# Ten and seven edge columns instead of eight and five for a tile of a relational graph layer

## The reference

```python
msgs = x[src]
out = x @ root + bias
for r in range(8):
    mask = (edge_type == r).astype(x.dtype)
    sums = jax.ops.segment_sum(msgs * mask[:, None], dst, num_segments=n)
    cnt = jax.ops.segment_sum(mask, dst, num_segments=n)
    out = out + (sums / jnp.maximum(cnt, 1.0)[:, None]) @ weight[r]
```

## Time and profile before

| | |
|---|---|
| three runs | 1642.74, 1644.76, 1646.51 us |
| profiled execution | 1644.54 us, its span 1642.8 us |
| PE busy | 1554.4 us (95% of the span), 7138 matmuls |
| VectorE busy | 890.7 us (54%) |
| GpSimd busy | 809.8 us (49%) |
| ScalarE busy | 406.0 us (25%) |
| items | 180: 130 planes (1580), 50 left-over columns (1564) |
| granted clock of PE | 0.987 of full speed over the span |

### The profile page before, as it was taken

How to read it: one execution, slowest core, us unless ns; L and a number is a source line. 1 busy time by engine, 2 the same in 40 slices (tenths; PEclk the granted TensorE clock), 3 DMA queues, 4 the chain that set the end, 5 groups by cost and what they waited for, 6 DMA issues and landing times.

```text
span 1642.8 us, 19045 instructions
## 1 busy us (share of the span) xinstructions
PE 1554.4 (95%) x7138; PEld 1259.3 (77%) x7138; DVE 890.7 (54%) x1334; ACT 406.0 (25%) x595; POOL 809.8 (49%) x682
## 2 busy tenths in 40 slices
PE   4999999999999999999999999999999879997988
PEld 4987777777778678888887888888777758876887
DVE  6535222444442320003888888884667656877785
ACT  3321112222222112122222222222211123232320
POOL 4426766667663136545555565654655634232220
PEclk9999999999999999999999999999999989998999
DMA  4422323333333222226777788877889874540001
GB/s 160 144 89 80 92 79 94 108 98 102 95 90 112 71 78 99 84 88 222 263 254 255 245 276 281 278 242 240 301 285 317 287 257 163 186 148 0 39 39 49
DMA packets 120459, 262.48 MB, mean 160 GB/s; under 512 B 23451, under 2 KB 37010, under 8 KB 120360
## 3 DMA queue, kind: packets, MB, share of 16 engines
q1 hardware_dynamic: 48568, 109.34, 19.9%
q0 software_dynamic: 33056, 83.02, 16.6%
q10 hardware_dynamic: 38736, 68.83, 11.3%
HBM read 193.33 MB, written 80.06 MB: 166 GB/s over the span
## 4 chain that ended last, share of the span: by engine, by line
PE 63%; DVE 16%; issue 8%; DMA 6%; POOL 3%; ACT 2%; ACTq 0%; POOLq 0%; SPq 0%; DVEq 0%
PE ps L1831 49%; DMA source_rows<-relation_rows,row_list 6%; PE ps L2074 5%; PE ps L2083 2%; DVE u_sum L1580 2%; PE ps L1958 1%; PE ps L1914 1%; PE ps L1938 1%; PE ps L1950 1%; POOL source_rows L922 1%; POOL xf L1025 1%; DVE u_sum L1590 1%; ACT source_rows_hi L2292 1%; PE ps L2144 1%; DVE xf L1726 1%
## 5 line engine op out<-in xcount | busy, mean ns | idle before, releaser
L1831 PE MATMUL ps<-WH,XTH 128*128 128x512 f32 (+1 forms) x1680 | 666.9, 397 | 0.0
L1831 PE MATMUL ps<-WH,XTL 128*128 128x512 f32 (+1 forms) x1680 | 652.6, 388 | 0.0
L1831 PE MATMUL ps<-WL,XTH 128*128 128x512 f32 (+1 forms) x1680 | 652.5, 388 | 0.0
L864 POOL TENSOR_TENSOR WL<-RAW,WH 128x512 fp32r<-128x512 f32 (+1 forms) x184 | 243.6, 1327 | 289.4 <-ACT WH L2210 286.4
L1831 PEld LDWEIGHTS ps<-WH,XTH 128*128 128x128 f32 x1680 | 318.4, 190 | 65.6 <-issue 7.1
L1831 PEld LDWEIGHTS ps<-WH,XTL 128*128 128x128 f32 x1680 | 316.7, 189 | 64.8
L1831 PEld LDWEIGHTS ps<-WL,XTH 128*128 128x128 f32 x1680 | 317.6, 189 | 60.7 <-issue 2.4
L922 POOL DMA_INDIRECT source_rows<-relation_rows,row_list x180 | 221.6, 1231 | 235.4 <-DVE u_sum L1580 130.7
L2232 ACT ACTIVATE EV<-ps 128x512 f32<-128x512 f32 x180 | 107.6, 598 | 631.6 <-PE ps L1831 543.2
L943 POOL DMA_INDIRECT edge_lists<-edge_words x160 | 196.9, 1231 | 46.4 <-issue 44.2
L1580 DVE SCALAR_TENSOR_TENSOR u_sum<-source_rows,weight_list,u_sum 128x1024 f32<-128x1024 f32 x120 | 165.4, 1378 | 60.8 <-DMA source_rows<-relation_rows,row_list 55.7
(11 more groups left out here) (312 smaller groups left out, 1499.9 us busy)
## 6 DMA issues: line engine op xcount, KB each, us to landing
relation_rows<-EV ACTq DMA_DIRECT2D x160, 256.0 KB
RAW<-in_L_gnn_weight SPq DMA_DIRECT2D x128, 256.0 KB
u_rows<-u_sum SPq DMA_DIRECT2D x20, 512.0 KB
RAW<-in_L_gnn_w_gate SPq DMA_DIRECT2D x32, 256.0 KB
mix_rows<-mix_rows_out ACTq DMA_DIRECT2D x10, 512.0 KB, 2.6
root_rows<-EV ACTq DMA_DIRECT2D x20, 256.0 KB
u_sum<-u_rows SPq DMA_DIRECT2D x10, 512.0 KB
bias_rows<-root_rows SPq DMA_DIRECT2D x10, 512.0 KB, 6.5
```

Of the source, the lines that this page charges most:

```text
L864: g.tensor_tensor(WL[:, h % 2, k, 0:w], RAW[:, q % 4, 0:w], WH[:, h % 2, k, 0:w].bitcast(F32), ALU.subtract).then_inc(w_lo, 1)
L1831: mm = t_.matmul(ps[:, bank, 0:w], a[:, t, k, :], b[:, s, k, 0:w], start=(k == 0 and j == 0), stop=(k == KT - 1 and j == 2))
```

## The change

Two tuples change. Everything that is computed from them moves with them: the number of items (130 + 50 = 180 becomes 170 + 30 = 200), the columns of the lists (180 becomes 200), the places of the left-over columns in a tile (0 and 6 of 12 in the first group, 0 of 8 in the second), the step of every item and of every fetch, and `COUNTED_AT` (88 becomes 85).

```diff
-PLANES = (8, 5)
-OVER = (3, 2)
+PLANES = (10, 7)
+OVER = (2, 1)
```

## The result

The change makes the kernel 0.8% slower: 1658.5 us, median of 7 runs (1653.0 to 1663.1), against 1645.5 for the kernel before in the same session; the ratio is 1.0082, 95% interval 1.0067 to 1.0098, +13 us. The forecast was 1640.2 with a range up to 1655. The profiled execution of the changed kernel took 1661.1 us, its span is 1659.3, 16.5 us longer than that of before.

What follows compares the result with a forecast made beforehand. PE was taken to bound most of the first group, the items the second. -2.9 - 5.9 + 1.5 + 1.0 + 2.0 = -4.3 us on 1644.5 gave 1640.2 us; range 1626 to 1655, the forecast's own 1635 to 1646.

Steps and rivals of the forecast that it cites:

- Counting, -2.9: Counting of left-over edges: 20 of 50 small PE matmuls go, all on the path, -2.9 us.
- PE's part, -5.9: First group, 881 to 1113 us: 6.3 left-over columns go where PE is the bound, -5.9 us.
- VectorE in the first group, +1.5 and +1.0: First group's added VectorE work: +1.5 us of PE waits from 881 to 1113, +1 us from 750 to 881.
- my sign for a wrong reading: First group's end shifting over 3 us against 9 us of PE work saved would prove that stretch misread.
- The fetches and the four slots in the second group, +2: Second group: 20 more fetches for the same rows through four slots, +0.2 us a tile, +2 us; ends -33 and +31.
- the long way round: Second group: a slot's 11.5 us from release after the second plane to use of its rows; as bound, +0.7 us a tile.
- the rest of the tile: Second group: the removed column's 1.9 us of VectorE and its waits go there, counting where another way is the bound.
- the first rival: Second group: slots become the bound twice a tile, group grows by 15 us, 1653 us; smaller form 1646; chance 0.29.
- My upper end of +31: Second group: if each fetch keeps its 3.09 us share, a tile takes 24.7 us, ten tiles +31 us.
- Moves the wait and doesn't add one: Group's end: seven planes, not three, follow the last left-over column; PE waits at the end instead, no added time.
- The rule: Fixed 2.0 us a DMA: 20 more fetches bring 40 us, 10 us with four in flight; sum would be 1643.
- The second (VectorE the bound of the first group, 0.08): First group: VectorE becomes the bound, 5.9 us lost and 3 us added, 1648 us; chance 0.08.

Runs made afterwards that it cites:

- the blocks cut: 24 quantizing blocks on VectorE cut to 16 of 352 columns: 1635.3 us on the changed kernel, 1639.4 us on the kernel before.
- the emptied fetches: Full change, four slots, with fetches of the first group's ninth and tenth and second group's sixth and seventh planes moving almost no rows: 1651.1 us.

## Why the prediction was wrong, step by step

The sum was -4.3 us and the spans differ by +16.5. Of the 20.8 us between them 12.2 lie in the first group, 8.2 in the second and 0.4 in the start.

**Counting, -2.9.** Right: 20 matmuls, 2.9 us.

**PE's part, -5.9, and VectorE in the first group, +1.5 and +1.0.** These three make -3.4; measured +8.8, and my sign for a wrong reading came, the group's end moved by 6.2 us. PE's columns did go (with the blocks cut, the first group fell from 360.0 to 350.6, the 9.3 us of ten columns). The step that failed is "what it needs is about ... 217.5 of 226 us. That holds on the mean". I compared VectorE's total with the stretch, and left out the slots in this group altogether; I had named the blocks that bunch VectorE's work and priced them at 1.5. The runs put in its place: 24 blocks of 4.4 to 7.3 us stop all releases, four slots cover no more than four items, and the loop's 7.3 us from release to landed begin again behind them. With 12 items a tile the group loses 23.5 us against PE's need, where 11 items lost 5.4, and a fifth slot gives 14 of them back. That there is no time between blocks to catch up is how I read this; one place of the trace was followed.

**The fetches and the four slots in the second group, +2.** Measured +8.7 in nine tiles and 1.5 at the end. The step that failed is the last one: I had +0.7 us a tile from the long way round, and let "the rest of the tile" give back nearly all, to +0.2. A tile grew by 0.97 (21.58 to 22.55). The long wait did not settle at the sixth plane: the longest of a tile stands there in four tiles and at the fourth, fifth or seventh plane in the others, and is 5.0 us or more in four of ten; two such waits in a tile, the sign of the first rival, show in none, but there are 21 waits and not 13. I took off 0.5 us for 31 fewer edges. By the emptied fetches this was too much: 1202 rows less gave this group 7 us, 0.006 us a row and not 0.017. What a tile saves elsewhere helps little where slots turn round twice a tile. The mean loop of the earlier trace rows was there to be read: seven items in 21.6 us with four slots is 12.3 us a loop. My upper end of +31 took this loop as fixed; it shortened from 12.45 to 11.53 us, 0.7 since rows wait less for VectorE and 0.6 since they land sooner, against 0.4 lost in the release and the fetch.

**"Moves the wait and doesn't add one"** at the end of the group: 1.5 us, small.

**The rule** of the Trainium skill ("DMA: Bandwidth & Descriptors", "Anatomy of one DMA — SWDGE (gpsimd) path"), about 2.0 us fixed in a DMA: the trace agrees in one place, where an empty tenth plane lands 1.88 us behind its instruction, and shows more in the three others (3.15, 5.57 and 4.50 us). It is a sixth of the loop, and priced alone it gave 1643.

**The rivals.** The first (slots the bound, second group +15, chance 0.29) is what the second group did, at two thirds of its price. The second (VectorE the bound of the first group, 0.08) came at the same time and cost more than its 3 us; its sign as I wrote it, VectorE without idle time, did not show. The range failed because I let only one of them happen at a time, though both feed on the same added items.

## What to carry to other kernels

Before items are added to a ring, read the loop of a slot from the trace (release, issue, landing, turn, use), divide by the slots, multiply by the new number of items, and compare that with the stage, in every stage that uses the ring. A block of other work on the consumer of the ring can count twice, once as work and once as a latency that starts again behind it, when it is longer than the slots can cover: here 24 blocks cost 23.5 us with four slots and 12 items a tile. Trading matrix work for items pays where the number of items stays (9, 5 with 2, 2: -5 us with four slots, and -11 with five, 1631.2 to 1619.8). A slot more (4 KB a partition) gave -14 us before the change and -29 after it, and with it the change neither pays nor costs (1631.2 and 1629.0).

## What the runs showed of the hardware

A gather's time from the end of its instruction to the landing hardly follows its rows. In the first group of the changed kernel the first left-over column of a tile (128 rows) takes 4.3 us, the second (27 on the mean) 4.5, the tenth plane (68) 3.7; emptied, that plane takes 1.9, but the second group's sixth plane still 5.6.

VectorE's short operations can stretch where GpSimd computes: here 0.34 us becomes 1.85 (L572, 352 columns), and GpSimd's L864 runs inside it. VectorE, stretched and not, and then GpSimd in the changed kernel:

```profile
995.56 1.85 DVE L572 TENSOR_SCALAR wq_tmp<-wq_rows 128x352 int32<-128x352 int32 x1
...
1015.62 0.34 DVE L572 TENSOR_SCALAR wq_tmp<-wq_rows 128x352 int32<-128x352 int32 x1
```

```profile
995.91 1.29 POOL L864 TENSOR_TENSOR WL<-RAW,WH 128x512 fp32r<-128x512 f32 x1
```

The operations of the 24 blocks are 32 us above their medians in sum, before and after the change alike, and over 31 of them in operations that lie beside a GpSimd operation of this kind. That is a quarter of the 130 us they take. The Trainium skill ("SBUF — State Buffer", "🔬 SBUF: two separate sides") says that the two engines share a port pair as an exclusive lock, which whichever starts first keeps for its whole instruction. The trace agrees that VectorE is held until GpSimd is done (it ends 0.2 us behind it), but not on the order: by its row VectorE's operation started 0.35 us before GpSimd's.

What stays open: with five slots the second group is still 11 us above PE's need with 7 items and 22 us with 8. In the kernel with 8 its granted clock is 0.94 where the first group's is 1.00; how much of that time is the lower clock after PE's idle times was not separated. Nor was what VectorE and GpSimd cost each other in the blocks separated from the held-up releases.
